# Two transformer layers on one core: jobs of the second layer interleaved into the first

## Chip, core and metric

One Trainium2 chip (trn2), one of its cores. The metric is the device time of one execution in microseconds (us); lower is better. Engines: PE multiplies matrices, DVE and ACT work on vectors, POOL is a slower vector engine, SP only issues DMAs.

## The reference

Four batches x of 256 tokens by 256 channels pass through two layers. LN has no weights; S = 256, D = 256.

```python
# layer 0: 32 query heads on 8 kv heads, head size 8
x = LN(x + softmax(q k^T / sqrt(8)) v Wo)            # q = x Wq, k = x Wk, v = x Wv
x = LN(x + (silu(x G * gs) * (x U * us)) Dn * ds)    # G, U: 256x768, Dn: 768x256, rounded to float8
# layer 1: 16 query heads on 8 kv heads, head size 16, weights transposed
x = LN(x + softmax(q k^T / 4) v wo^T)
g = lut[gate_idx]; u = lut[up_idx]; d = lut[down_idx]    # 688x256, 688x256, 256x688, lut of 16 floats
x = LN(x + (silu(x g^T) * (x u^T)) d^T)
```

## The kernel before

**Jobs.** A job is one batch through one layer: jobs 0 to 3 are layer 0, jobs 4 to 7 layer 1, and job j takes batch j % 4 (`layer`, L53). Job 4 + b needs the output of job b. X (the four batches in fp32) stays on the chip.

**Written orders.** `ORDER` (L68 to L195) holds for PE, ACT, DVE, POOL and SP a list of steps, written out word by word. Each engine runs its list strictly in this order, and steps of different engines are tied by semaphores. A step is `kind.job.part`, and on PE `@n` names one of the three FB banks of PSUM that the step fills. So what an engine does next is fixed; a step whose inputs are late holds up all behind it on its engine.

**The steps of a job, with the lines.**
- `q`, `kv` (PE L948, L966, L971): projections of XT, x transposed, in two buffers; `ldxt` on SP loads them for layer 0, `tr.j.1` (PE L1089, ACT L659) makes them for layer 1 from the finished X. ACT, DVE and POOL split q and k into three bf16 parts (`q`, `qmid`, `kv`, `kmid`), and SP stacks the parts along the partitions (`qstack.j.0` to `.2`, L468, six DMAs; `kstack`, L475, six): QS and KS have NST = 3 buffers, so the stack of job j waits for the scores of job j - 3.
- `max` (PE L992 into MM, DVE L813): the row maxima of the scores, 16 steps a job in layer 0 and 8 in layer 1. There is one MM: the matmuls of a step wait for the reduction of the last. `mt.j.0/1` (DVE L824, L826; PE L1001; ACT L649; SP L511) turns the maxima into two more rows of the stack, for half of the scores each.
- `score` (PE L1024 into SC, ACT L691 exp into PB): 16 or 8 steps, one SC, so the matmuls of one wait for the exp of the last. In layer 0, a step is two matmuls of 512 columns, of two kv groups whose keys lie in partitions 0 to 63 and 64 to 127. PB holds 6 units of exps.
- `pv` (PE L1041 in layer 0, L1050 in layer 1): four strips of 32 rows. Part 0 of a region waits for all the exps of the region (in layer 0 four scores). `stage` (ACT L709), `turn` (PE L1063, DVE L839, L840), `back` (PE L1071, ACT L699): division by the sums, and back.
- `wo` (PE L1080; DVE L851, then the norm's statistics, L772 and L777; POOL L570 to L574 normalizes X). `tr.j.0` (PE L1089, ACT L656, DVE L883) makes XH and XL, the high and low part of the transposed x.
- `gu.j.i.w` (PE L1108): chunk i of six of gate (w = 0) or up (w = 1). Layer 0 has four matmuls in such a step, layer 1 six, since its weights too have a high and a low part. The chunk then goes through ACT (tanh, L682), DVE (L874, L877, into HF, two buffers), ACT (HH, L667) and POOL (HL = HF - HH, `hsplit`, L581).
- `down.j.i` (PE L1119): four matmuls in layer 0, six in layer 1. Its norm is that of `wo`; in layer 0, DVE first multiplies by DS in two instructions (L861).
- `out.j` (SP L527).

**Weights of layer 0's FFN** are rounded through float8 in 12 blocks (`ldq8`, `q8`, `q8w`) into W0. **Weights of layer 1's FFN** are decoded in ten blocks of 432 columns: `ldix` (SP), `lutix` and `lutbits` (ACT, DVE), `lut1` (POOL L599), `lut2` to `lut4` (DVE L919) pick the value by the index bits in LV; `lutlow` copies the high part to W1 (ACT L741), subtracts (POOL L588) and writes the low part to dw in DRAM (SP L523). When all ten are there, `reload` (ACT L742 to L746) fetches dw over W0, once layer 0's FFNs are done: it waits for `down_ready` = 4. The first gu of layer 1 waits for it (`low_in`).

**The places in the orders** that the prediction speaks of. In PE's list before, job 3's FFN stands around max.5.5 and max.5.6, and job 4's begins after max.7.0. In SP's list before: `... qstack.3.2 qstack.3.1 qstack.3.0 mt.1.0 ...` and `... kstack.7.1 lutlow.9 kstack.7.2 mt.6.0 ...`. In ACT's list: `... mt.6.0 reload stage.5.1 score.6.0 ...`.

Of the kernel before, what the change touches and what calls it, by code (L numbers as in the profile page):

```python
# [1175 lines left out]
```

## Time and profile before

| | us |
|---|---|
| median of 3 runs | 384.27 (382.66 to 386.99) |
| the profiled execution | 384.53 |
| its span, first to last instruction | 382.6 |
| PE busy (x instructions) | 309.3 (x2464) |
| DVE busy | 288.5 (x510) |
| ACT busy | 217.0 (x391) |
| POOL busy | 160.9 (x245) |

The granted clock of PE was 0.915 of its full speed over the span; in the slices it is 5 to 9 tenths in the first 155 us and 9 or more behind. Matmuls are pipelined and the records of neighbours overlap, so PE's busy time is more than what its instructions take. A record of a matmul in fp32 comes twice (two passes), of one in fp32r or bf16 once. Times in the rows are us from the start of the span.

### The profile page before, as it was taken

The numbers are of one execution on the slowest core, as the hardware profiler recorded it, in microseconds if no ns is written. First come the engines' busy times: TensorE is split into PE (matmuls) and PEld (weight loads), VectorE is DVE, ScalarE is ACT, GpSimd is POOL, SyncE is SP. The second block draws the span as 40 slices with busy tenths as digits, with TensorE's granted clock in tenths as the row PEclk, the third lists the DMA queues.
The fourth block names the chain that finished last, engine by engine and source line by source line (L and its number), as shares of the span: only waits on it lengthen the run. The fifth ranks groups of instructions, "written<-read, shape, count | busy, mean of one in ns | idle before, by whom it ended". The sixth has DMA issues, their size and how long they took to land.

```text
span 382.6 us, 7048 instructions
## 1 busy us (share of the span) xinstructions
PE 309.3 (81%) x2464; PEld 197.7 (52%) x2464; DVE 288.5 (75%) x510; ACT 217.0 (57%) x391; POOL 160.9 (42%) x245
## 2 busy tenths in 40 slices
...
GB/s 204 291 180 127 148 95 41 40 10 133 14 57 2 11 39 2 69 17 90 2 3 95 55 27 2 78 72 3 10 140 232 3 3 0 3 30 0 29 29 27
DMA packets 23491, 23.06 MB, mean 60 GB/s; under 512 B 3348, under 2 KB 23316, under 8 KB 23328
## 3 DMA queue, kind: packets, MB, share of 16 engines
...
## 4 chain that ended last, share of the span: by engine, by line
PE 39%; DVE 14%; ACT 12%; SPq 12%; issue 10%; POOL 8%; DMA 4%; DVEq 0%; POOLq 0%; ACTq 0%
PE FB L1108 12%; PE FB L1119 7%; PE SC L1024 5%; ACT PB L691 5%; DVE MX L813 5%; SPq L475 4%; SPq L468 4%; PE MM L992 4%; PE FB L1080 3%; PE PV L1041 2%; DVE LV L919 2%; POOL LV L599 2%; POOL X L574 2%; DMA QS<-MP 2%; DVE HF L877 2%
## 5 line engine op out<-in xcount | busy, mean ns | idle before, releaser
L813 DVE TENSOR_REDUCE MX<-MM 128x4 f32<-128x1024 f32 x96 | 117.0, 1219 | 27.9 <-PE MM L992 21.8
L691 ACT ACTIVATE PB<-SC 128x1024 f32<-128x1024 f32 x96 | 98.0, 1021 | 43.9 <-PE SC L1024 40.4
L992 PE MATMUL MM<-KS,QS 62*128 62x256 bf16 (+1 forms) x384 | 48.9, 302 | 26.6 <-DVE MX L813 26.1
L581 POOL TENSOR_TENSOR HL<-HF,HH 128x256 fp32r<-128x256 f32 (+1 forms) x48 | 35.6, 745 | 64.7 <-ACT HH L667 64.4
L599 POOL TENSOR_SCALAR LV<-LB,LD,LT 128x432 f32<-128x432 f32 x80 | 56.2, 717 | 12.8 <-ACT LB L736 12.7
L1024 PE MATMUL SC<-QS,KS 64*128 64x512 bf16 (+1 forms) x192 | 47.6, 418 | 17.3 <-ACT PB L691 11.0
L1108 PE MATMUL FB<-XH,W 128*128 128x256 f32 x288 | 54.8, 299 | 0.2
L992 PEld LDWEIGHTS MM<-KS,QS 62*128 62x128 bf16 (+1 forms) x384 | 20.0, 99 | 55.0 <-DVE MX L813 43.0
L1108 PEld LDWEIGHTS FB<-XH,W 128*128 128x128 f32 x288 | 41.6, 190 | 6.8 <-issue 3.4
L1041 PE MATMUL PV<-PB,VP 128*32 128x256 f32 x512 | 42.3, 433 | 1.9 <-ACT PB L691 1.9
L919 DVE COPY_PREDICATED LV<-LB,LV 128x432 f32<-128x432 uint8 x70 | 42.2, 663 | 2.1 <-POOL LV L599 1.2
L1108 PE MATMUL FB<-XL,W 128*128 128x256 f32 x192 | 38.7, 283 | 0.0
L1024 PEld LDWEIGHTS SC<-QS,KS 64*128 64x128 bf16 (+1 forms) x192 | 10.6, 96 | 43.0 <-ACT PB L691 24.2
L874 DVE SCALAR_TENSOR_TENSOR AA<-TH,FB 128x256 f32<-128x256 f32 (+1 forms) x48 | 19.9, 415 | 15.3 <-ACT TH L682 11.3
L1119 PE MATMUL FB<-W,HH 128*128 128x256 f32 (+1 forms) x144 | 30.2, 307 | 0.4 <-POOL HL L581 0.4
L1108 PEld LDWEIGHTS FB<-XL,W 128*128 128x128 f32 x192 | 29.8, 191 | 0.1
L667 ACT ACTIVATE HH<-HF 128x256 fp32r<-128x256 f32 (+1 forms) x48 | 19.6, 413 | 14.7 <-DVEq L879 12.1
L588 POOL TENSOR_TENSOR LO<-LV,W 128x432 f32<-128x432 f32 x10 | 11.5, 1146 | 38.3 <-ACT W L741 38.3
L1119 PEld LDWEIGHTS FB<-W,HH 128*128 128x128 f32 (+1 forms) x144 | 21.8, 193 | 6.7 <-issue 2.6
L948 PE MATMUL FB<-XT,WQ 128*128 128x256 f32 x64 | 19.3, 448 | 4.1 <-issue 4.1
L574 POOL TENSOR_SCALAR X<-X,NM,RSTD 128x256 f32<-128x256 f32 x32 | 21.2, 670 | 1.7
L1041 PEld LDWEIGHTS PV<-PB,VP 128*32 128x32 f32 x512 | 12.9, 116 | 16.7 <-issue 11.2
...
## 6 DMA issues: line engine op xcount, KB each, us to landing
QS<-QP SPq DMA_DIRECT2D x48, 128.0 KB, 2.4
IX<-in_idx SPq DMA_DIRECT2D x10, 216.0 KB, 3.2
dw<-LO SPq DMA_DIRECT2D x10, 216.0 KB, 1.9
W<-dw ACTq DMA_DIRECT2D x1, 2160.0 KB, 8.8
...
```

Of the source, the lines that this page charges most:

```text
L574: ins = pool.tensor_scalar(X[:, j % B, t, :], X[:, j % B, t, :], NM[:, n % 2, t:t + 1], RSTD[:, n % 2, t:t + 1], ALU.add, ALU.mult)
L581: pool.tensor_tensor(HL[0:r, i, :], HF[0:r, c % 2, :], HH[0:r, i, :].bitcast(F32), ALU.subtract).then_inc(h_parts, 1)
L599: ins = pool.tensor_scalar(LV[:, i, :], LB0[:, :], LD[:, i:i + 1], LT[:, 2 * i:2 * i + 1], ALU.mult, ALU.add)
L691: act.activation(PB[:, unit % PB_UNITS:unit % PB_UNITS + 2, kt, :, :], SC[:, :, :].rearrange("p (f e) s -> p f e s", f=2), ACT.Exp, scale= ...
L813: dve.tensor_reduce(mx, MM[:, :, :].rearrange("p (f i) s -> p f i s", f=2), axis=AX.X, op=ALU.max).then_inc(max_red, 1)
L874: link(dve.scalar_tensor_tensor(out=AA[0:r, :], in0=TH[0:r, (6 * j + i) % 2, :], scalar=1.0, in1=bank[0:r, 0:S], op0=ALU.add, op1=ALU.mult))
L919: ins = dve.copy_predicated(LV[:, i, :], LB[:, k, :], LV[:, i + gap, :])
L992: ins = pe.matmul(MM[:, 2 * f + i, :], QS[lo:lo + r, j % NST, qs + h, qt * P:(qt + 1) * P], keys(j)[lo:lo + r, j % NST, ks, :], start=True ...
L1024: ins = pe.matmul(SC[:, 2 * f:2 * f + 2, :], keys(j)[lo:lo + r, j % NST, ks, kt * P:(kt + 1) * P], QS[lo:lo + r, j % NST, qs + h:qs + h + ...
L1041: ins = pe.matmul(PV[32 * c:32 * c + 32, r % 2, :], VP0[:, j % NST, kt, 4 * (r // 2) + c, w:w + 32], PB[:, (first + c) % PB_UNITS, kt, e, ...
L1108: ins = pe.matmul(bank[:, w * S:(w + 1) * S], ffn_up(l, w, t, i)[part], xs[:, t, :], start=k == 0, stop=k == len(products) - 1)
L1119: ins = pe.matmul(bank[:, t * D:(t + 1) * D], hs[0:rows(l, i), i, t * P:(t + 1) * P], ffn_down(l, i)[part], start=i + k + t == 0, stop=(i, ...
```

## The change

1. Jobs run in the order of `SEQ`: batches 0, 1, 2 of layer 0, batch 0 of layer 1, batch 3 of layer 0, batches 1, 2, 3 of layer 1. So job 3 is now layer 1's batch 0 (it needs job 0), job 4 is layer 0's batch 3, and jobs 5, 6, 7 need jobs 1, 2, 4. All orders are rewritten for it.
2. XT has three buffers.
3. dw is fetched into a tile of its own, W1L, which lies over LV and IX, the scratch of the decoding; `reload` no longer waits for `down_ready`. Q8A and Q8B lie in AA.
4. A score step of layer 0 takes one query head of each of four kv groups: four matmuls of 256 columns. PB holds three quads, and `pv` waits for the exps of its own quad; part order in layer 0 is (quad, kt) instead of (kt, half).

```diff
-PB_UNITS = 6
+PB_QUADS = 3
+SEQ = ((0, 0), (0, 1), (0, 2), (1, 0), (0, 3), (1, 1), (1, 2), (1, 3))
+NXT = 3
 def layer(j):
-    return j // B
+    return SEQ[j][0]
+def batch(j):
+    return SEQ[j][1]
+def earlier(j):
+    return SEQ.index((0, batch(j)))
...
     "PE": (
...
+        "pv.4.3.1 mt.5.0@2 q.6.0@0 score.4.15 q.6.1 back.4.0@2 max.5.5 pv.4.3.2 pv.4.3.3 max.5.6 wo.4.0@1 score.5.0 "
+        "turn.4.1@2 max.5.7 score.5.1 pv.5.0.0 back.4.1@0 score.5.2 pv.5.0.1 mt.5.1@2 wo.4.1 score.5.3 gu.3.0.0@0 "
+        "gu.3.0.1 gu.3.1.0@2 gu.3.1.1 gu.3.2.0@1 gu.3.2.1 gu.3.3.0@0 gu.3.3.1 gu.3.4.0@2 gu.3.4.1 gu.3.5.0@1 gu.3.5.1 "
+        "tr.4.0@0 max.6.0 down.3.0@2 down.3.1 down.3.2 gu.4.0.0@1 gu.4.0.1 down.3.3 down.3.4 max.6.1 score.5.4 "
+        "down.3.5 gu.4.1.0@0 gu.4.1.1 gu.4.2.0@1 gu.4.2.1 gu.4.3.0@2 gu.4.3.1 max.6.2 score.5.5 pv.5.1.0 down.4.0@0 "
+        "gu.4.4.0@1 gu.4.4.1 down.4.1 max.6.3 down.4.2 gu.4.5.0@2 gu.4.5.1 score.5.6 down.4.3 pv.5.1.1 down.4.4 "
+        "score.5.7 max.6.4 turn.5.0@1 down.4.5 pv.5.2.0 pv.5.2.1 pv.5.3.0 pv.5.3.1 max.6.5 mt.6.0@2 back.5.0@0 "
+        "turn.5.1@1 wo.5.0@2 tr.4.1@0 back.5.1@1 max.6.6 score.6.0 q.7.0@0 q.7.1 kv.7.0@1 kv.7.1 max.6.7 score.6.1 "
+        "pv.6.0.0 wo.5.1 score.6.2 mt.6.1@0 pv.6.0.1 score.6.3 pv.6.1.0 pv.6.1.1 max.7.0 tr.5.0@1 score.6.4 "
...
     "ACT": (
...
+        "score.4.14 lutlow.9 mt.5.0 score.4.15 q.6 back.4.0 reload qmid.6 stage.4.1 score.5.0 score.5.1 back.4.1 "
...
     "DVE": (
...
+        "tr.3.0 max.5.3 kv.6 mt.5.0 lut4.9 max.5.4 turn.4.0 max.5.5 q.6 max.5.6 turn.4.1 max.5.7 mt.5.1 wo.4 gu.3.0 "
+        "gu.3.1 gu.3.2 gu.3.3 gu.3.4 gu.3.5 tr.4.0 max.6.0 gu.4.0 max.6.1 down.3 gu.4.1 gu.4.2 max.6.2 gu.4.3 gu.4.4 "
+        "max.6.3 gu.4.5 mt.6.0 max.6.4 down.4 turn.5.0 max.6.5 turn.5.1 max.6.6 q.7 max.6.7 kv.7 mt.6.1 wo.5 max.7.0 "
...
     "SP": (
+        "load.0 ldq8.0 ldq8.1 ldxt.1 load.1 ldix.0 ldxt.2 ldix.1 load.2 ldix.2 qstack.0.0 ldq8.2 ones kstack.0.0 "
+        "qstack.0.1 kstack.0.1 qstack.0.2 kstack.0.2 ldq8.3 ldxt.4 ldix.3 ldq8.4 qstack.1.0 kstack.1.0 kstack.1.1 "
...
+        "mt.1.0 lutlow.3 ldix.7 mt.1.1 lutlow.4 ldix.8 mt.2.0 kstack.3.0 qstack.3.0 qstack.3.1 qstack.3.2 kstack.3.1 "
...
+        "mt.4.1 kstack.6.0 kstack.6.1 kstack.6.2 mt.5.0 lutlow.9 qstack.6.0 qstack.6.1 qstack.6.2 mt.5.1 out.3 mt.6.0 "
+        "qstack.7.0 qstack.7.1 kstack.7.0 qstack.7.2 kstack.7.1 kstack.7.2 mt.6.1 mt.7.0 mt.7.1 out.5 out.6 out.7 "
...
-        XT = sb("XT", [P, 2, DT, S])
-        PB = sb("PB", [P, PB_UNITS, 2, 2, S])
+        XT = sb("XT", [P, NXT, DT, S])
+        PB = sb("PB", [P, PB_QUADS, 2, 4, S])
...
+        spare = ExitStack()
+        LV = spare.enter_context(nc.sbuf_tensor("LV", [P, 8, LUT_W], F32))
+        IX = spare.enter_context(nc.sbuf_tensor("IX", [P, 2, LUT_W], I32))
+        spare.close()
+        W1L = sb("W1L", [P, W1_COLS], F32R)
...
+        def place(j, c):
+            return 2 * (c % 2) + c // 2 if layer(j) == 0 else c
...
                 elif kind == "score":
                     _, j, v = step
-                    unit, kt = unit0(j) + 2 * (v // 2), v % 2
-                    if unit >= PB_UNITS:
-                        act.wait_ge(pv_mm, region_of(unit + 1 - PB_UNITS) + 1)
+                    quad, kt = quad0(j) + v // 2, v % 2
+                    if quad >= PB_QUADS:
+                        act.wait_ge(pv_mm, quad - PB_QUADS + 1)
...
                 elif kind == "reload":
                     act.wait_ge(dw_wr, 16 * N_LUT)
-                    act.wait_ge(down_ready, B)
-                    act.dma_start(W0[:, 0:W1_COLS].bitcast(F32), dw).then_inc(low_in, 16)
+                    act.dma_start(W1L[:, :].bitcast(F32), dw).then_inc(low_in, 16)
...
-                    for f in range(2):
-                        if layer(j) == 0:
-                            g, h = 2 * (2 * (u // 4) + u % 2) + f, 2 * (u // 2 % 2)
-                        else:
-                            g, h = 2 * u + f, 0
-                        lo, ks, qs = stacked(j, g)
-                        ins = pe.matmul(SC[:, 2 * f:2 * f + 2, :],
-                                        keys(j)[lo:lo + r, j % NST, ks, kt * P:(kt + 1) * P],
-                                        QS[lo:lo + r, j % NST, qs + h:qs + h + 2, :], start=True, stop=True)
+                    if layer(j) == 0:
+                        for c in range(4):
+                            lo, ks, qs = stacked(j, 4 * (u // 4) + c)
+                            ins = pe.matmul(SC[:, place(j, c), :], keys(j)[lo:lo + r, j % NST, ks, kt * P:(kt + 1) * P],
+                                            QS[lo:lo + r, j % NST, qs + u % 4, :], start=True, stop=True)
...
                 elif kind == "pv":
...
-                    if part == 0:
-                        pe.wait_ge(exp_done, first + per)
...
+                        e, kt = part // 2, part % 2
+                        quad = quad0(j) + 2 * r + e
...
+                        kt, quad = part, quad0(j) + r
+                    pe.wait_ge(exp_done, 2 * quad + kt + 1)
...
+                    if kt == 1:
+                        ins.then_inc(pv_mm, 1)
```

## Rows read from the trace of the kernel before

**Rows 1.** Page, part 1: busy us (share of the span) and instructions of each engine.

```profile
PE 309.3 (81%) x2464; PEld 197.7 (52%) x2464; DVE 288.5 (75%) x510; ACT 217.0 (57%) x391; POOL 160.9 (42%) x245
```

**Rows 2.** Windows; columns: stretch, length, busy us (x instructions), PEclk, DMA, GB/s.

```profile
24.60:258.00 233.40, 184.22 (x1506) 98.23 (x1506) 200.58 (x334) 152.70 (x264) 100.22 (x142) 0.88 0.19 53
258.00:295.10 37.10, 29.74 (x251) 21.00 (x250) 27.71 (x53) 18.09 (x31) 16.07 (x24) 0.95 0.30 99
295.10:314.00 18.90, 18.62 (x157) 13.86 (x156) 14.79 (x25) 9.96 (x18) 5.09 (x9) 1.00 0.01 3
314.00:375.70 61.70, 61.41 (x507) 53.90 (x505) 30.70 (x76) 26.63 (x57) 25.21 (x45) 1.00 0.04 14
```

**Rows 3.** Chain that ended last, from 340 us on: start, us, what.

```profile
340.35 1.43 PE PV L1050 x24
...
362.49 8.72 PE FB L1108 x72
371.21 4.51 PE FB L1119 x36
...
375.74 0.70 DVE X L864
```

**Rows 4.** Timeline of PE, layer 1: start, us, line, op, tiles, count.

```profile
290.51 0.60 PE L992 MATMUL MM<-KS,QS 96*128 96x256 bf16 x4
...
291.38 1.03 PE L1080 MATMUL FB<-WO,ON 128*128 128x256 f32 x4
```

**Rows 5.** Timeline of PE, layer 0.

```profile
187.93 0.39 PE L992 MATMUL MM<-KS,QS 62*128 62x256 bf16 x4
188.16 0.38 PE L1024 MATMUL SC<-QS,KS 64*128 64x512 bf16 x2
188.47 0.44 PE L1071 MATMUL FB<-IDN,NT 128*128 128x128 f32 x2
```

**Rows 6.** Lines of DVE by form: busy us, mean ns, idle before.

```profile
L813 DVE TENSOR_REDUCE MX<-MM 128x4 f32<-128x1024 f32 x96 | 117.0, 1219 | 27.9 <-PE MM L992 21.8 <-DVE HF L877 3.4
...
L874 DVE SCALAR_TENSOR_TENSOR AA<-TH,FB 128x256 f32<-128x256 f32 x44 | 18.3, 415 | 13.0 <-ACT TH L682 8.9 <-POOL HL L581 2.1 <-DVE HF L877 1.6
...
L861 DVE TENSOR_TENSOR FB<-FB,DS 128x256 f32<-128x256 f32 x8 | 3.0, 421 | 0.3 <-PE FB L1119 0.3
```

**Rows 7.** Timeline of SP at the start.

```profile
14.55 1.95 SPq L468 DMA_DIRECT2D QS<-QP  x3
...
23.43 1.51 SPq L481 DMA_DIRECT2D KS<-KS  x2
```

**Rows 8.** Timeline of SP around mt.1.0 and mt.6.0.

```profile
86.26 3.88 SPq L468 DMA_DIRECT2D QS<-QP  x6
...
285.55 0.67 SPq L511 DMA_DIRECT2D QS<-MP  x1
```

**Rows 9.** Timeline of PE: score.1.0 and score.6.0, idle before in brackets.

```profile
92.90 0.61 PE L1024 MATMUL SC<-QS,KS 64*128 64x512 bf16 x2 [0.96 <-DMA QS<-MP]
...
287.56 1.03 PE L1024 MATMUL SC<-QS,KS 98*128 98x512 bf16 x2 [2.90 <-DMA QS<-MP]
```

**Rows 10.** Waits of PE from 64 to 300 us: total, times, longest.

```profile
PE SC L1024 <- ACT PB L691: 9.4, 18, 1.2
```

**Rows 11.** DMA issues: count, KB each, median us to landing.

```profile
QS<-QP SPq DMA_DIRECT2D x48, 128.0 KB, 2.4
...
dw<-LO SPq DMA_DIRECT2D x10, 216.0 KB, 1.9
W<-dw ACTq DMA_DIRECT2D x1, 2160.0 KB, 8.8
```

**Rows 12.** Timeline of ACT: reload and the step behind it.

```profile
286.46 0.34 ACTq L746 DMA_DIRECT2D W<-dw  x1
286.90 0.60 ACT L709 ACTIVATE ST<-PV 128x512 f32<-128x512 f32 x1 [4.86 <-DMA dw<-LO]
```

**Rows 13.** Timeline of DVE in the FFN block of job 3.

```profile
255.44 0.42 DVE L874 SCALAR_TENSOR_TENSOR AA<-TH,FB 128x256 f32<-128x256 f32 x1 [1.28 <-POOL HL L581]
```

More of the change, by code:

```diff
@@ L45, with later, first @@
 W1_COLS = N_LUT * LUT_W
+SEQ = ((0, 0), (0, 1), (0, 2), (1, 0), (0, 3), (1, 1), (1, 2), (1, 3))
+NXT = 3
 def layer(j):
-    return j // B
+    return SEQ[j][0]
[3 more added lines that the diff above has]
+    return SEQ.index((0, batch(j)))
+def later(j):
+    return SEQ.index((1, batch(j)))
+def first(l):
+    return min(j for j in range(JOBS) if layer(j) == l)
 def halves(j):
@@ L277, in two_layer_kernel @@
         RAW = sb("RAW", [P, 2, Q8_W])
-        Q8A = sb("Q8A", [P, Q8_W], FP8)
-        Q8B = sb("Q8B", [P, Q8_W], FP8)
+        Q8A = AA[:, :].bitcast(FP8)[:, 0:Q8_W]
+        Q8B = AA[:, :].bitcast(FP8)[:, Q8_W:2 * Q8_W]
         BIG = sb("BIG", [P, Q8_W], I32)
@@ L312, in two_layer_kernel @@
         dw = nc.dram_tensor("dw", (P, W1_COLS), F32, kind="Internal").ap()
-        ld_xt = [sem(f"ld_xt{i}") for i in range(2)]
+        ld_xt = [sem(f"ld_xt{i}") for i in range(NXT)]
         ld_w0 = sem("ld_w0")
@@ L392, in stack_count, with xt_count, quad0 @@
             return 16 * NPROD * (j // NST + 1)
+        def xt_count(j):
+            return 16 * sum(layer(i) == 0 for i in range(j % NXT, j + 1, NXT))
         def rows_count(n):
             return 16 * sum(halves(i // 2) for i in range(n % 2, n + 1, 2))
-        def region_of(unit):
-            first = unit0(B)
-            return unit // 4 if unit < first else 4 * B + (unit - first) // 2
+        def quad0(j):
+            return unit0(j) // 2
         def ffn_up(l, which, dt, i):
             o = which * DT * (I0, I1)[l] + dt * (I0, I1)[l] + i * P
-            return (W0[:, o:o + P],) if l == 0 else (W1[:, o:o + P], W0[:, o:o + P])
+            return (W0[:, o:o + P],) if l == 0 else (W1[:, o:o + P], W1L[:, o:o + P])
         def ffn_down(l, i):
@@ L621, in _ @@
                     act.wait_ge(kv_ready, j + 1)
-                    if j in (0, B):
-                        act.wait_ge(ones_pool, 1 if j == 0 else 2)
+                    if j == first(l):
+                        act.wait_ge(ones_pool, l + 1)
                     if j >= NST:
-                        act.wait_ge(pv_mm, 4 * (j - NST + 1))
+                        act.wait_ge(pv_mm, quad0(j - NST + 1))
                     for kt in range(2):
@@ L704, in _ @@
                     n = 2 * j + p
-                    act.wait_ge(pv_mm, 2 * (n + 1))
+                    act.wait_ge(pv_mm, quad0(j) + UNITS[layer(j)] // 4 * (p + 1))
                     if n >= 2:
@@ L937, in _ @@
                     _, j, m = step
-                    l, b = layer(j), j % 2
+                    l, b = layer(j), j % NXT
                     if m == 1:
@@ L1010, in _ @@
                         pe.wait_ge(m_rows[m % 2], rows_count(m))
-                    if v == 0 and j == B:
+                    if v == 0 and j == first(1):
                         pe.wait_ge(ones_in, 16 * 2)
```

92 lines of the change are left out of this document (44 added, 48 removed), and 211 rows, old and new, of the table ORDER.

## The prediction

> **What bounds the kernel now.** I read the page's totals, then a windows view cut at four max steps, then the tail's chain, the timelines around what moves, and the waits. By the page no engine is full: PE 81% of the span, DVE 75% [rows 1]. That is an average over two regimes. To see them I cut where PE starts max.0.0 (24.6 us), max.5.7 (258.0), max.7.0 (295.1) and max.7.7 (314.0) [rows 2]. A, 24.6 to 258.0: DVE busy 200.6 of 233.4 us, PE 184.2. B, to 295.1: DVE 27.7 of 37.1, PE 29.7. C, to 314.0: PE 18.6 of 18.9. D, to 375.7: PE 61.4 of 61.7, DVE half idle. So DVE and the exchange between engines bound A, and PE alone bounds D. A gain lies in PE work that leaves D and finds cover under DVE work. By the written order D holds 38 gu and 24 down steps of layer 1, six matmuls each.
>
> **Prices.** Matmuls overlap, so busy time is no price; I take distances between starts where nothing is waited for. Layer 1: gu 8.72 us for 72 matmuls, 12 steps, = 0.73; down 4.51 for 6 = 0.75; pv 1.43 for 3 = 0.48 [rows 3]; a max and a score step together 0.87 (290.51 to 291.38) [rows 4]. Layer 0: max 0.23, score 0.31 [rows 5]; gu and down, of four matmuls, two thirds of layer 1's. DVE: max 1.22, of which 0.08 lies over its neighbour; an FFN chunk 0.42 and as much again [rows 6]; a norm 1.7 (375.74 to some 377.4 [rows 3]), in layer 0 two multiplies by DS of 0.42 more. PE's small steps are taken in the same way. With these I add up both written orders between the four landmarks, in us of PE work and of DVE work:
> A: before 136 and 193.5, after 132 and 191.6.
> B: before 25.4 and 22.1, after 44.2 and 30.8.
> C: before 16.9 and 13.9, after 15.3 and 11.9.
> D: before 57.7 of PE, after 44.5.
> The totals are the same. The change takes 13 us of PE work out of D (10 gu, 6 down, one each of pv, score, tr, turn) and puts 19 into B, where all of job 3's FFN (12 gu, 6 down of layer 1) and of job 4's (as many of layer 0) now stand.
>
> **A, -5.8.** (1) Order: 191.6 for 193.5 of DVE work at A's own rate, 233.4/193.5 = 1.21: -2.3. (2) Start: SP now issues ldq8.2 and the two `ones` loads between qstack.0.0 and kstack.0.0. Job 0's stack keeps SP busy from 14.55 to 22.3, and max.0.0 starts 2.3 us behind; the `ones` alone take 1.51 [rows 7]. X, 1 MB, also goes out ahead of IX, on whose conversion SP waits. I take +2.5, ends 0 and +5. (3) mt.1.0 stood on SP behind six qstack.3 issues, 86.26 to 90.14 [rows 8], and score.1.0 waited for it until 92.90 [rows 9]; now job 3's stack comes later. PE's own idle was 0.96, the delay 3.88: -2, ends 0 and -3.9. (4) pv now asks for one quad's exps, not for a region's four scores, and an exp's buffer is free after one pv_mm of its own quad. From 64 to 300 us PE waited 9.4 us for exps ahead of scores [rows 10]. Ends 0 and -9.4; -4, nearer none, since a score still waits for the one SC. (5) Layer 0's score step is now four matmuls of 256 columns over two row groups, not two of 512. Its like is layer 0's max, 0.23 from start to start against 0.31 [rows 5]: 0, ends -5 (64 x 0.08) and, if the row groups ran one after the other at twice 0.23, +10 of PE time, most of it under DVE. (6) The third XT buffer, Q8A and Q8B in AA and W1L in LV and IX add no instruction and, with the orders as written, no wait of their own (AA's first gu comes long after q8.11, and reload waits for dw anyway): 0.
>
> **B, +17.4.** PE's 44.2 exceed DVE's 30.8: the stretch turns from DVE-bound to PE-bound. At D's rate, 61.7/57.7, put at 1.06: 46.9. Two stalls on top.
> First, `reload`. From lut4.9 on: ACT's copy 0.6, POOL 1.15, SP 0.6 to 1.3, landing in dw 1.9, then 2160 KB in 8.8 [rows 11]: 13.4 us. PE's list from there to gu.3.0.0 holds 7.4 us of work, four scores with their exps in series among it, some 10.5 in all: a stall of 2.5, ends 0 and 6. Queued behind gu.3.0.0 are max.6.0 and all of PE, and DVE waits for both. Today PE doesn't wait for these weights, though ACT stood 4.86 us for dw [rows 12]. The wait for down_ready goes, as W1L is not W0; only so can reload come ahead of job 3's FFN.
> Second, job 7's chain, which now hangs on job 4. From down.4.5: DVE's norm 2.6, POOL's 2.4, then tr.4.1, with turn.5.0 (and so back.5.0) behind that norm; PE has 3.9 us of steps ahead of tr.4.1, so 2 with the hand-overs. Then q.7 to max.7.0: twelve stack issues at 0.65 (six in 3.88 [rows 8]) from q_hi on, which is 2.4 us in, and 2.4 of landing [rows 11]: 12.6. PE's q and kv, and three scores with their exps, fill some 9.5: 3.1. Together 5.1, ends 2 and 8. Behind max.7.0 stand tr.5.0 and gu.5, so all of PE waits here too.
> B after: 46.9+2.5+5.1 = 54.5, against 37.1. The 2.90 us ahead of score.6.0, for mt.6.0 behind kstack.7 on SP [rows 8, 9], are in the 37.1 only: mt.6.0 now precedes qstack.7.0.
>
> The new reload runs on ACT's queue while SP sends six qstack.6 loads of 128 KB; beside today's there are none. If they share the engines' time, reload lands later by what the stacks move: 768 KB at 2160/8.8 = 245 KB/us, 3.1 us [rows 11]. That is the third rival. The Trainium skill ("DMA: Bandwidth & Descriptors", Queues, rings and completion order) says that each DMA engine goes round its queues packet by packet, which would make it so; no stretch of this trace shows it for the reload.
>
> **C, -1.8; D, -12.8.** C: 15.3 at today's 18.9/16.9 = 17.1. D: 44.5 at 1.065 = 47.4, and 1.5 for tr.6.0, over whose norm (DVE 1.7, POOL 2.4, hand-overs) only 3.9 us of PE steps lie: 48.9 against 61.7. The chain through mt.7.1, four scores, pv, turn, wo, tr and gu.7 needs some 37, so it is no bound. Behind the last matmul nothing changes: 6.9 us to the end of the span.
>
> **The sum.** -5.8+17.4-1.8-12.8 = -3.0. The profiled execution took 384.53 (its span 382.6 and 1.9 around it); the median of the runs is 384.27. So 381.5 for such an execution and 381.2 for the median, -0.8%. Under 1%, 3.8 us, is about what a measurement of this kernel can't tell from no change.
>
> **Rivals.**
> First, the moved work hides. PE is idle for 49 us of A, DVE for 9 of B [rows 2]. If B's FFN steps fill waits rather than add to them, B grows by 10, not 17.4: 373.8; at the most all of D's 12.8 is gained, 371.5. For it: D runs gap-free with the same steps. Against: the twelve gu steps of job 3 stand in one block with no max between, so DVE starves. The Trainium skill ("Perfetto Trace Analysis", Identifying the Most-Contended Engine) says that interleaving regimes with different busiest engines may help; it doesn't say by which of the two prices.
> Second, slower: in B the hand-over of FFN chunks sets the pace, not PE. A chunk goes PE, ACT, DVE (0.42 twice), ACT, POOL, over three banks and two HF buffers, with maxes of 1.22 between on DVE; layer 0's costs PE only 0.96. It decides from a rate of 1.13 in B on (3.0/44.2 above 1.06), where the gain is gone. Today's B ran at 37.1/25.4 = 1.46, stalls and all; midway, at 1.25, it costs 8.4: 389.6. For it: DVE waited 1.28 us for POOL's HL in the like block at 255 [rows 13]. Against: D has the same hand-over and runs at 1.07.
> Third, reload lands 3.1 us later: 384.3, no change.
> Fourth, the change doesn't do what it says, in that the scores' row groups lose their overlap: +10 of PE time, a fifth of which A lets through: 383.2.
>
> **Chances.** Forecast 0.42, first rival 0.26, second 0.18, third 0.09, fourth 0.05. The forecast's own range is 377 to 386; as it lies near the 1% bound (380.4), 0.17 of it is faster, 0.23 same, 0.02 slower. First: 0.24 faster, 0.02 same. Second: 0.14 slower (over 388.1), 0.04 same. Third and fourth: 0.01 faster, 0.11 same, 0.02 slower. Faster 0.42, same 0.40, slower 0.18. The range goes from the first rival's full hiding, 371, to just past the second, 391.
>
> **What would show it.** Right: the last max starts at 323 to 328 (today 314) and PE is solid for 48 to 50 us behind it; gu.3.0.0 waits 1 to 4 us for reload; max.7.0 waits 2 to 4 for stack 7; score.1.0 no longer waits for rows; layer 0's score steps stand 0.23 to 0.31 apart. Wrong: A is shorter by over 10 us; or B takes under 47 us (the work hid) or over 58 (the hand-over or reload decides). DVE's idle time ahead of max.6.x and its releaser tell which.

## The result, and the profile after

| | before | after |
|---|---|---|
| median of the runs, us | 384.17 (4 runs) | 397.65 (396.14 to 399.94, 4 runs) |
| ratio, 95% interval | 1 | 1.034 (1.029 to 1.039) |
| the profiled execution, us | 384.53 | 397.33, span 395.5 |

The change made the kernel 3.4% slower; the forecast was 381.2 in a range of 371 to 391. The time is outside the range and on the other side of 1.

The page of after, part 1 (compare [rows 1]), and part 2's row of the granted clock in 40 slices of 9.9 us:

```profile
PE 313.6 (79%) x2592; PEld 199.1 (50%) x2592; DVE 285.0 (72%) x510; ACT 217.1 (55%) x391; POOL 161.5 (41%) x245
...
PEclk9966558798699989999999999996999989999998
```

The totals hardly moved: DVE has 3.5 us less, PE 4.3 more, the span is 12.9 longer. So the time is in waits and in where they lie. The clock row has two dips behind 155 us, in slices 28 and 33, which [rows 2] don't have to that depth (0.95 and 1.00).

The windows of after, cut where PE starts the same four steps as in [rows 2] (max.0.0, max.5.7, max.7.0, max.7.7):

```profile
28.20:261.60 233.40, 182.83 (x1615) 95.08 (x1616) 201.09 (x336) 147.51 (x255) 106.04 (x147) 0.89 0.19 53
261.60:320.60 59.00, 50.70 (x396) 39.39 (x394) 33.23 (x70) 28.05 (x53) 19.48 (x35) 0.94 0.22 68
320.60:339.60 19.00, 18.24 (x140) 13.89 (x140) 12.77 (x20) 8.84 (x15) 1.46 (x2) 0.92 0.01 2
339.60:388.60 49.00, 48.10 (x394) 40.82 (x392) 23.67 (x60) 21.30 (x46) 20.25 (x36) 1.00 0.04 13
```

Against the stretches of before:

| | before | after | moved by | forecast |
|---|---|---|---|---|
| up to max.0.0 | 24.6 | 28.2 | +3.6 | +2.5, told in A |
| A | 233.4 | 233.4 | 0 | -8.3 (-5.8 with the start) |
| B | 37.1 | 59.0 | +21.9 | +17.4 |
| C | 18.9 | 19.0 | +0.1 | -1.8 |
| D | 61.7 | 49.0 | -12.7 | -12.8 |
| sum | | | +12.9 | -3.0 |

The sum misses by 15.9: 9.4 of it ahead of the end of A, 4.5 in B, 1.9 in C, 0.1 in D. The first cut of before was taken a little early: its PE starts max.5.7 at 258.38, not at 258.0. So 0.4 us of A stand in B in the column of before, and by the exact cut A lost 0.4 and B gained 22.3; the tables and sums below keep 258.0.

**Where B's time went.** The timeline of PE in after, at the first gu of layer 1 (columns as in [rows 4], the idle time before in brackets):

```profile
270.51 0.77 PE L1139 MATMUL FB<-XH,W 128*128 128x256 f32 x2 [3.59 <-DMA W1L<-dw]
271.08 0.63 PE L1139 MATMUL FB<-XH,W1L 128*128 128x256 f32 x2
271.51 0.63 PE L1139 MATMUL FB<-XL,W 128*128 128x256 f32 x2
...
275.35 0.63 PE L1139 MATMUL FB<-XL,W 128*128 128x256 f32 x2
275.77 0.50 PE L1139 MATMUL FB<-XH,W 128*128 128x256 f32 x2
276.11 0.40 PE L1139 MATMUL FB<-XH,W1L 128*128 128x256 f32 x2
276.35 0.40 PE L1139 MATMUL FB<-XL,W 128*128 128x256 f32 x2
```

Read the distances between starts. Behind a wait of 3.59 us for the reload, a pair of matmuls takes 0.43 us; from 276.11 on it takes 0.235. The first twelve pairs (270.51 to 275.77, 5.26 us) thus cost 12 x (0.43 - 0.235) = 2.3 us more than the same work behind them. Windows of these 5.26 us and of as many behind them say why (PEclk is the third column from the end):

```profile
270.51:275.77 5.26, 5.26 (x24) 5.26 (x25) 0.85 (x2) 0.38 (x1) 0.31 (x1) 0.50 0.02 6
276.10:281.30 5.20, 5.20 (x47) 5.20 (x46) 3.08 (x8) 2.68 (x8) 2.45 (x4) 1.00 0.00 0
```

The granted clock is 0.50, the lower of PE's two levels (1.2 of 2.4 GHz), and then 1.00. It fell during PE's wait of 3.59 us, over which it is 0.81 on average. The wait costs 5.9, not 3.6.

The kernel before has the same thing, at its wait of 2.90 us ahead of score.6.0. The prediction's rows show it: two matmuls of 512 columns of that step take 1.03 us [rows 9], while four of 256 columns at the end of the slow stretch take 0.60 [rows 4]. The window of the 3 us from score.6.0 on:

```profile
287.50:290.50 3.00, 2.94 (x12) 2.43 (x13) 0.56 (x2) 1.30 (x3) 0.00 (x0) 0.50 0.89 317
```

The reload itself, and the queue beside it (DMA issues, as in [rows 11]; then SP's timeline and ACT's issue):

```profile
W1L<-dw ACTq DMA_DIRECT2D x1, 2160.0 KB, 10.9
```

```profile
258.03 5.01 SPq L502 DMA_DIRECT2D QS<-QP  x6
...
259.45 0.34 ACTq L782 DMA_DIRECT2D W1L<-dw  x1
```

It landed in 10.9 us where 8.8 was seen in [rows 11], and the six qstack issues beside it took 5.01 where six took 3.88 [rows 8]. That W1L is another tile than W0 isn't the reason: in the run code_only below, the same transfer into W1L has no stack loads beside it and lands in 9.0 (in one profiled execution, of 389.31 us).

PE and DVE at the second place, max.7.0, the first step of job 7:

```profile
316.12 0.61 PE L1063 MATMUL SC<-QS,KS 98*128 98x512 bf16 x2 [0.54 <-ACT PB L729]
...
317.90 0.64 PE L1083 MATMUL PV<-PB,VP 128*32 128x256 f32 x8 [0.60 <-ACT PB L729]
320.62 1.01 PE L1028 MATMUL MM<-KS,QS 96*128 96x256 bf16 x4 [2.09 <-issue]
321.43 1.06 PE L1120 MATMUL FB<-IDN,X 128*128 128x128 f32 x4
322.28 1.06 PE L1063 MATMUL SC<-QS,KS 98*128 98x512 bf16 x2
```

And DVE's own timeline at that place:

```profile
321.74 1.23 DVE L849 TENSOR_REDUCE MX<-MM 128x4 f32<-128x1024 f32 x1 [5.43 <-PE MM L1028]
```

PE waits 0.54 + 0.60 + 2.09 us around job 7's stack, and again the steps behind it are slow: 1.01 and 1.06 us where 0.60 stands in [rows 4]. "issue" names no releaser. SP's last three stack loads of job 7 were issued from 317.29 to 319.13, and such loads take some 2 us to land, so the stack is most likely what came last. DVE idles 5.43 us for it.

**Where A's time did not go.** Waits of PE in after, 64 to 300 us, as in [rows 10]. The scores of layer 0 and of layer 1 now have a line each, which before was one:

```profile
PE SC L1058 <- ACT PB L729: 9.5, 13, 1.8
PE SC L1063 <- ACT PB L729: 0.6, 3, 0.2
```

10.1 us, against 9.4 before: the finer release of the exps, put at -4, bought nothing.

DVE is busy for 201.1 us of A; before, 200.6 [rows 2], although the prediction counted 1.9 us less work. That is a matter of the cut. PE and DVE don't reach a step together: before, PE started max.5.7 at 258.38 and DVE reduced it only at 262.22, behind gu.3.4, gu.3.5, lutbits.9 and turn.4.0 (3.33 us busy from 258.0 to 262.22). In after, PE starts it at 261.59 and DVE reduces it at 262.75, with only turn.4.1 between. Cut at DVE's own max.0.0 and max.5.7, before and after:

```profile
25.00:262.22 237.22, 188.07 (x1548) 101.36 (x1548) 203.91 (x343) 153.98 (x267) 102.19 (x145) 0.88 0.18 52
29.18:262.75 233.57, 183.18 (x1616) 95.34 (x1616) 201.27 (x338) 147.25 (x251) 106.18 (x147) 0.90 0.19 54
```

DVE did lose 2.6 us of work and comes through its part 3.6 us faster, but PE gets none of it: between PE's own two starts A is as long as before.

At score.1.0, whose wait for rows (0.96 us [rows 9]) is gone, PE now waits one step earlier and longer, for DVE's reduction of max.1.9, ahead of which DVE's list has mt.1.0 and wo.0:

```profile
96.41 0.61 PE L1028 MATMUL MM<-KS,QS 62*128 62x256 bf16 x4 [2.42 <-DVE MX L849]
97.15 0.61 PE L1058 MATMUL SC<-QS,KS 64*128 64x256 bf16 x4
```

PE starts score.1.0 27.4 us behind max.1.0 (69.75); before, it was 27.2 (92.90 behind 65.73).

### The profile page after: what moved, and what is told of

Its sections match the earlier page's. It is cut to its first block, busy times and chain, and to the rows that moved or that the text cites. A ratio compares the mean times of both kernels' runs of the same rounds, so it can differ in the third digit from the quotient of the medians.

```text
span 395.5 us, 7309 instructions
## 1 busy us (share of the span) xinstructions
PE 313.6 (79%) x2592; PEld 199.1 (50%) x2592; DVE 285.0 (72%) x510; ACT 217.1 (55%) x391; POOL 161.5 (41%) x245
## 4 chain that ended last, share of the span: by engine, by line
PE 38%; DVE 17%; issue 11%; ACT 9%; SPq 8%; POOL 8%; DMA 8%; DVEq 0%; POOLq 0%; ACTq 0%
PE FB L1139 12%; PE FB L1150 6%; DVE MX L849 5%; ACT PB L729 4%; PE MM L1028 3%; SPq L509 3%; DMA W1L<-dw 3%; POOL X L608 3%; PE SC L1058 3%; PE PV L1083 3%; PE FB L1111 2%; DVE HF L913 2%; POOL LV L633 2%; DMA IX<-in_idx 2%; DVE LV L955 2%
## 5 line engine op out<-in xcount | busy, mean ns | idle before, releaser
L1083 PE MATMUL PV<-PB,VP 128*32 128x256 f32 x768 | 62.3, 405 | 2.6 <-ACT PB L729 2.3
L1139 PE MATMUL FB<-XH,W 128*128 128x256 f32 x192 | 44.0, 312 | 4.1 <-DMA W1L<-dw 3.6
L955 DVE COPY_PREDICATED LV<-LB,LV 128x432 f32<-128x432 uint8 x70 | 43.2, 678 | 0.2
L1139 PEld LDWEIGHTS FB<-XH,W 128*128 128x128 f32 x192 | 31.3, 199 | 12.2 <-issue 7.5
L1058 PE MATMUL SC<-QS,KS 64*128 64x256 bf16 x256 | 27.0, 292 | 12.4 <-ACT PB L729 10.7
L1139 PEld LDWEIGHTS FB<-XL,W 128*128 128x128 f32 x192 | 30.9, 198 | 0.0
L1083 PEld LDWEIGHTS PV<-PB,VP 128*32 128x32 f32 x768 | 16.5, 110 | 25.1 <-issue 16.6
L1058 PEld LDWEIGHTS SC<-QS,KS 64*128 64x128 bf16 x256 | 8.3, 96 | 30.5 <-ACT PB L729 22.7
L720 ACT ACTIVATE TH<-FB 128x256 f32<-128x256 f32 (+1 forms) x24 | 9.2, 382 | 26.3 <-PE FB L1139 26.2
L1150 PE MATMUL FB<-W,HH 128*128 128x256 f32 (+1 forms) x96 | 21.6, 307 | 1.1 <-DVEq L916 1.0
L984 PE MATMUL FB<-XT,WQ 128*128 128x256 f32 x64 | 20.3, 466 | 0.5 <-DVE QR L826 0.5
## 6 DMA issues: line engine op xcount, KB each, us to landing
W1L<-dw ACTq DMA_DIRECT2D x1, 2160.0 KB, 10.9
```

Source lines behind the costliest of these rows:

```text
L955: ins = dve.copy_predicated(LV[:, i, :], LB[:, k, :], LV[:, i + gap, :])
L984: ins = pe.matmul(bank[:, m * S:(m + 1) * S], WQ[l][:, t, m:D:2], XT[:, b, t, :], start=t == 0, stop=t == DT - 1)
L1058: ins = pe.matmul(SC[:, place(j, c), :], keys(j)[lo:lo + r, j % NST, ks, kt * P:(kt + 1) * P], QS[lo:lo + r, j % NST, qs + u % 4, :], star ...
L1083: ins = pe.matmul(PV[32 * c:32 * c + 32, r % 2, :], v, PB[:, quad % PB_QUADS, kt, place(j, c), :], start=part == 0, stop=part == (3, 1)[la ...
L1139: ins = pe.matmul(bank[:, w * S:(w + 1) * S], ffn_up(l, w, t, i)[part], xs[:, t, :], start=k == 0, stop=k == len(products) - 1)
L1150: ins = pe.matmul(bank[:, t * D:(t + 1) * D], hs[0:rows(l, i), i, t * P:(t + 1) * P], ffn_down(l, i)[part], start=i + k + t == 0, stop=(i, ...
```

## The experiments

All ratios are to runs of the kernel before on the same chip in the same rounds.

**The new code under the old orders (code_only).** `SEQ` is the natural order and all lists are those of before, while quads, buffers and W1L are the change's.

```diff
-SEQ = ((0, 0), (0, 1), (0, 2), (1, 0), (0, 3), (1, 1), (1, 2), (1, 3))
+SEQ = ((0, 0), (0, 1), (0, 2), (0, 3), (1, 0), (1, 1), (1, 2), (1, 3))
 ORDER = {
-    ...
+    the lists of the kernel before
```

> The changed code (score quads, one quad's exps ahead of pv, three XT buffers, W1L over the scratch, reload without down_ready) under the old job order and all five old written orders. Theory 1 (the job order with its written orders is what costs; the code is neutral): 382 to 386 us, A (first max to max.5.7) 231 to 235 us. Theory 2 (the quads cost: four short matmuls a score, more wait handling ahead of pv, and this ate the gain forecast for A): 388 us or more, A at 238 or more.

388.01 us, ratio 1.003 (0.999 to 1.007). The median is outside the 382 to 386 of the first theory and at the bound of the second, but the kernel before ran at 385.43 on this chip, so the ratio decides: by its interval the code costs 0.7% at the most and gains 0.1%, and most of the 3.4% comes from the orders. The -4 for quads goes. The fourth rival, the lost overlap of row groups, was priced at 2 us or 0.5%, which this interval doesn't exclude; the trace of after does. A score step of layer 0 stands 0.32 us ahead of the next step, where 0.31 was seen before [rows 5] and 0.46 would be twice 0.23:

```profile
255.86 0.39 PE L1058 MATMUL SC<-QS,KS 64*128 64x256 bf16 x4
256.18 1.14 PE L984 MATMUL FB<-XT,WQ 128*128 128x256 f32 x4
```

**The reload in two DMAs (split_reload).** The first brings what gate and up read, the second what down reads, which waits for it separately.

```diff
-act.dma_start(W1L[:, :].bitcast(F32), dw).then_inc(low_in, 16)
+cut = 2 * DT * I1 + P
+act.dma_start(W1L[:, 0:cut].bitcast(F32), dw[:, 0:cut]).then_inc(low_in, 16)
+act.dma_start(W1L[:, cut:].bitcast(F32), dw[:, cut:]).then_inc(low_in2, 16)
...
+                    if j == first(1) and i == 0:
+                        pe.wait_ge(low_in2, 16)
```

> The changed kernel, with the reload issued as two DMAs, the gate and up columns first with a semaphore of their own; the down columns are waited for before down.3.0. Theory 1 (the stall ahead of gu.3.0.0 costs twice: 3.6 us of waiting and some 3.3 us because PE's granted clock is at the lower level for the next five gu steps): the load of the first part lands in some 7 us instead of 10.9, gu.3.0.0 starts 3.5 us sooner without a wait, its steps take 0.72 at once, total 391 us. Rival (the FFN block is bound by its hand-overs, the stall is hidden by what comes later, at max.7.0): 396 or more.

393.72 us, ratio 1.022 (1.016 to 1.028), so 1.2% of the 3.4 are gone; the time lies between the theory's 391 and the rival's 396. DMA issues and PE's timeline of this kernel:

```profile
W1L<-dw ACTq DMA_DIRECT2D x1, 1440.0 KB, 6.8
W1L<-dw ACTq DMA_DIRECT2D x1, 720.0 KB, 9.2
```

```profile
267.11 0.59 PE L1142 MATMUL FB<-XH,W 128*128 128x256 f32 x2
267.53 0.40 PE L1142 MATMUL FB<-XH,W1L 128*128 128x256 f32 x2
267.77 0.40 PE L1142 MATMUL FB<-XL,W 128*128 128x256 f32 x2
```

No bracket stands behind the first row: no wait, and no slow pairs. B is 52.4 long, 6.6 less than after's, which is the 5.9 read above and little else. C grew from 19.0 to 20.3 with a granted clock of 0.85, since the wait at max.7.0 is still there; part of the gain was lost to it.

**Filler matmuls in the reload's wait (warm).** The reload stays whole; thirty matmuls into a bank that the first gu then overwrites keep PE busy up to it.

```diff
+                            if j == 3:
+                                for n in range(30):
+                                    pe.matmul(bank[:, 0:S], W1[:, 0:P], XH[:, n % 2, :], start=True, stop=True)
                             pe.wait_ge(low_in, 16)
```

> The changed kernel, with 30 matmuls of 256 columns (some 3.6 us) that write what gu.3.0.0 then overwrites, put between score.5.3 and the wait for reload. The wait stays. Theory 1 (clock): gu.3.0.0 starts at the same time within 0.5 us, its first five steps take 0.72 and not 1.1 to 1.4 each, total 394.5. Rival (those steps are slow because something else holds them, the reload's DMA or the first weights): no step is faster, total 397.5 or more.

396.73 us, ratio 1.029 (1.024 to 1.034); by the median 0.5% below the change, with intervals that overlap, and between the theory's 394.5 and the rival's 397.5. The trace shows the mechanism where the median is weak:

```profile
267.52 3.94 PE L1134 MATMUL FB<-XH,W 128*128 128x256 f32 x30
271.30 0.40 PE L1142 MATMUL FB<-XH,W 128*128 128x256 f32 x2
271.53 0.40 PE L1142 MATMUL FB<-XH,W1L 128*128 128x256 f32 x2
```

The weights came no sooner than in the change (271.3 against 270.5), but the pairs are 0.235 apart from the first on. From the first gu to max.6.0 PE took 8.9 us instead of 11.4. So the two costs are separate: 3.6 for the wait and, by this run, 2.5 for the clock behind it (2.3 by the pairs above).

**SP's start as before (start_order).** IX's loads ahead of load.1, ldq8.2 and the ones behind job 0's stack.

```diff
-load.0 ldq8.0 ldq8.1 ldxt.1 load.1 ldix.0 ldxt.2 ldix.1 load.2 ldix.2 qstack.0.0 ldq8.2 ones kstack.0.0 qstack.0.1 kstack.0.1 ...
+load.0 ldq8.0 ldq8.1 ldxt.1 ldix.0 ldix.1 load.1 ldxt.2 load.2 ldix.2 qstack.0.0 kstack.0.0 kstack.0.1 qstack.0.1 ... ldq8.2 ones
```

> The changed kernel, with SP's list at the start as it was in the kernel before: IX ahead of X, ldq8.2 and ones behind job 0's stack. Theory 1: max.0.0 starts 3 us earlier (25.2 instead of 28.2) and all of it stays, as DVE bounds what follows: 394.5. Rival (the late start is given back in A, since max.5.7 is paced by the decoding): 397 to 398.

398.67 us, ratio 1.035 (1.029 to 1.041): no gain, a miss; the rival was nearer. PE started max.0.0 at 25.3 instead of 28.2, but max.1.0 at 69.8 instead of 69.7. DVE's list has q8.2 ahead of max.0.0, and its load was now late:

```profile
25.35 0.36 DVE L933 TENSOR_SCALAR BIG<-RAW 128x384 int32<-128x384 int32 x1 [8.74 <-DMA RAW<-in_gate]
```

**SP's, DVE's and ACT's start together (start_both).** The same, with q8.2 behind kv.1 in DVE's list and behind q.1 and kv.1 in ACT's.

```diff
-DVE: ... q8.1 q8.2 q.1 max.0.0 kv.1 q8.3 max.0.1 ...
+DVE: ... q8.1 max.0.0 q.1 kv.1 q8.2 max.0.1 lut2.0 q8.3 ...
-ACT: ... lutbits.0 q8.2 q.1 kv.1 q8w.2 ...
+ACT: ... lutbits.0 q.1 kv.1 q8.2 q8w.2 ...
```

> The changed kernel, with job 0's start put back in three lists at once: SP sends IX ahead of X and ldq8.2 and ones behind job 0's stack; DVE takes q8.2 and q8.3 behind max.0.0 and max.0.1 instead of ahead of them; ACT takes q.1 and kv.1 ahead of q8.2. Theory (the written order of job 0 on DVE, where max.0.0 stands behind q8.2, is what lost 4 us at max.1.0 and made the run start_order lose what it gained): max.0.0 at 25.3, max.1.0 at 66.5 to 67.5 instead of 69.7, total 394.5 to 395.5. Rival (job 0 is bound by its DVE work, start or not): max.1.0 at 69 or later, total 397 or more.

401.06 us, ratio 1.038 (1.032 to 1.044): a second miss, and again the rival's side. DVE now waited at max.0.0 itself, for job 0's stack:

```profile
25.75 1.22 DVE L849 TENSOR_REDUCE MX<-MM 128x4 f32<-128x1024 f32 x1 [9.53 <-PE MM L1028]
```

What DVE doesn't do ahead of the stack, it has to do later: max.1.0 started at 70.9, later than in the change itself. The earliest max.0.0 isn't the best start. Why max.4.0 to max.5.0 then took 52.3 us instead of 48.6 I can only say from the clock, 0.86 from 190 to 215 us where the change has 1.00; what lowered it stays open.

**Split reload and fillers ahead of max.7.0 (split_warm7).** Eighteen matmuls into MM behind the last reduction and ahead of the wait for job 7's stack.

```diff
+                    if j == 7 and u == 0:
+                        pe.wait_ge(max_red, unit0(j) + u)
+                        for n in range(18):
+                            pe.matmul(MM[:, 0, :], W1[:, 0:P], XH[:, n % 2, :], start=True, stop=True)
                     if u == 0:
                         pe.wait_ge(q_in[j % NST], stack_count(j))
```

> As split_reload, and 18 matmuls of 256 columns (some 2.1 us) into MM, which max.7.0 then overwrites, ahead of the wait for job 7's stack. Theory (a wait of 2 us there lowers PE's granted clock for the next steps, and C, at 20.3 us for 15.3 of work, pays for it): max.7.0 starts at the same time within 0.5 us, C takes 17.5 to 18.5 us, total 391.5 to 392.5. Rival (C is bound by DVE's reductions and exps, the clock doesn't matter): C stays at 20, total 393.5 or more.

391.69 us, ratio 1.013 (1.007 to 1.019), as the theory said. Windows of B and C:

```profile
264.20:316.70 52.50, 50.04 (x415) 39.30 (x413) 33.23 (x70) 27.61 (x53) 19.44 (x35) 1.00 0.23 74
316.70:334.50 17.80, 17.06 (x143) 12.85 (x142) 12.70 (x20) 8.85 (x15) 1.46 (x2) 1.00 0.01 2
```

The clock is 1.00 throughout, and C is 17.8 instead of 20.3. B and C together are 70.3 us against the change's 78.0 and the 56.0 of before. Job 7's stack is still waited for, now under 2.4 us of fillers; without them the sum would be 67.9, and still 11.9 above before. So without the two stalls B and C still take back nearly all of D's 12.7, and the later start is on top. By the prices, B and C have 17.2 us of PE work more than before; 11.9 of it shows in the time.

**Half of the gu work left out, in A and in B (trim_a, trim_b).** Both on top of the last kernel: in one the gu steps of jobs 0, 1 and 2, all in A, take only the first half of the 256 input channels; in the other those of jobs 3 and 4, all in B.

```diff
+                    full = len(products)
+                    if j in (0, 1, 2):          # the other kernel: (3, 4)
+                        products = [q for q in products if q[2] == 0]
```

> split_warm7 with the gu steps of jobs 0, 1 and 2 (all in stretch A) cut to half of their matmuls: the second half of the 256 input channels is left out, 36 steps x 2 matmuls x 0.12 us = 8.6 us of PE work gone from A. split_warm7 measured 391.7 (1.0134). If PE work in A lies under DVE's (201 busy of 233 us), as the price of nothing for the four us that left A says, A loses under 2 us: 390 to 392. Rival: A is set by the exchange PE-DVE in series, so PE work counts there at half or more: 383 to 387. A lower granted clock because PE does less could also make it slower, up to 393.

> split_warm7 with the gu steps of jobs 3 and 4 (all in stretch B) cut to half in the same way: 12 steps x 3 matmuls (layer 1) and 12 x 2 (layer 0), 60 x 0.12 = 7.2 us of PE work gone from B. If B is PE-bound, it loses nearly all of it: 385 to 386 (1.000 of the kernel before). Rival, the hand-over of FFN chunks or DVE's maxes set B's pace: the time stays within 2 us of split_warm7's 391.7.

In A: 391.93 us, ratio 1.020 (1.014 to 1.026); the median didn't fall, and the profiled A went from 235.7 to 233.2 us for 8.6 us of PE work taken away. PE work in A is nearly free, so the 4 us that the change took out of A could buy little.

In B: 389.76 us, ratio 1.012 (1.007 to 1.017), and the profiled B fell by 1.6, to 50.9: of 7.2 us of PE work, under a quarter came back. My expectation missed. Timeline of PE, DVE and POOL inside job 3's block in that kernel:

```profile
271.51 0.39 PE L1149 MATMUL FB<-XH,W 128*128 128x256 f32 x1 [0.39 <-DVEq L919]
...
272.71 0.39 PE L1149 MATMUL FB<-XH,W 128*128 128x256 f32 x1 [0.22 <-DVEq L919]
...
273.69 0.42 DVE L913 SCALAR_TENSOR_TENSOR AA<-TH,FB 128x256 f32<-128x256 f32 x1 [1.19 <-POOL HL L616]
...
274.79 0.39 PE L1149 MATMUL FB<-XH,W 128*128 128x256 f32 x1 [1.09 <-DVEq L919]
```

From the fourth chunk on PE now waits for DVE's release of the FB bank. Chunks come 1.20 us apart, and once 2.08, when POOL is at the norm of X and HL is late; from the first gu to max.6.0 it took 7.9 us. With all matmuls PE alone needs 1.42 a chunk, 9.1 us up to max.6.0, and it runs that block without a gap. So PE does set the pace of job 3's block, but the hand-over lies right behind it: the second rival's mechanism is there, one step down. In the rest of B the 2.9 us left out of job 4's gu bought 0.4; which step took their place there I haven't followed up. The price of PE work in B holds for work added to it, not for work taken out.

**The kernel before with what it waited for moved away (old_unblocked).** Here I left the change and asked which of its ideas were good alone: mt.1.0 ahead of the qstack.3 issues, mt.6.0 behind kstack.7.0 on SP, the reload split, and behind stage.5.1 and score.6.0 in ACT's list.

```diff
-SP:  ... lutlow.2 qstack.3.2 qstack.3.1 qstack.3.0 mt.1.0 ldix.6 ...
+SP:  ... lutlow.2 mt.1.0 qstack.3.2 qstack.3.1 qstack.3.0 ldix.6 ...
-SP:  ... kstack.7.0 qstack.7.2 kstack.7.1 lutlow.9 kstack.7.2 mt.6.0 mt.6.1 ...
+SP:  ... kstack.7.0 mt.6.0 qstack.7.2 kstack.7.1 lutlow.9 kstack.7.2 mt.6.1 ...
-ACT: ... mt.6.0 reload stage.5.1 score.6.0 back.5.0 ...
+ACT: ... mt.6.0 stage.5.1 score.6.0 reload back.5.0 ...
```

> The kernel before, job order untouched, with the waits that the trace shows taken out by small moves: mt.1.0 ahead of qstack.3 and mt.6.0 behind kstack.7.0 on SP, stage.5.1 and score.6.0 ahead of reload on ACT, reload in two DMAs. Theory (these rows come late and hold all of PE): score.1.0 1.5 to 2 us and score.6.0 2.5 us earlier, total 380 to 382. Rival (a step that comes earlier in A or B only waits longer for DVE later): 383.5 to 385.

381.51 us, ratio 0.987 (0.983 to 0.992): it beats both kernels. Windows of B, C and D:

```profile
257.40:291.40 34.00, 28.12 (x249) 19.56 (x248) 27.35 (x52) 17.88 (x30) 15.79 (x23) 1.00 0.28 88
291.40:311.10 19.70, 18.87 (x158) 13.83 (x157) 14.89 (x26) 9.97 (x18) 5.11 (x9) 1.00 0.09 37
311.10:372.70 61.60, 61.30 (x507) 53.82 (x505) 30.64 (x76) 26.66 (x57) 25.31 (x45) 1.00 0.04 14
```

B is 3.1 us shorter than in [rows 2], 2.7 by the exact cut at 258.38. The waits of PE's scores for rows of maxima, 6.1 us over the span of the kernel before (2.90 of them at score.6.0 [rows 9]), are down to:

```profile
PE SC L1027 <- DMA QS<-MP: 2.0, 3, 0.8
```

The reload is late here too, but costs only this:

```profile
292.48 0.71 PE L1111 MATMUL FB<-XH,W 128*128 128x256 f32 x4 [0.55 <-DMA W<-dw]
```

**Its parts (old_mt1, old_reload).** mt.1.0 alone, and the reload alone (split, and moved in ACT's list):

> The kernel before with one edit, mt.1.0 ahead of the six qstack.3 issues in SP's list (the step that the prediction put at -2, ends 0 and -3.9). Theory: worth the prediction's value, 0.3 to 0.7% faster (383 to 381.5 beside 384.3). Rival: the wait of score.1.0 lies beside DVE work in a stretch that DVE sets, and the time stays within 0.2%.

> The kernel before with the reload in two DMAs and behind stage.5.1 and score.6.0 in ACT's list, mt.1.0 and mt.6.0 left where they are. ACT then doesn't stand 4.86 us for dw ahead of two steps that PE and DVE wait for. Theory: ACT's wait held PE, 2 to 3 us gone: 0.5 to 0.8% faster. Rival: score.6.0 then waits on mt.6.0 (behind kstack.7 on SP, 2.90 us) all the same, and the time stays within 0.3%.

mt.1.0 alone: 382.66 us, ratio 0.991 (0.987 to 0.995). The forecast's -2 for this edit was right in sign and, at 1.9 to 5.0 us by the interval, not too large; the gain is above the 0.3 to 0.7% expected of this run, but the intervals overlap. The reload alone: 384.71, ratio 0.998 (0.994 to 1.002), nothing to be told from none. The rival of that run held: score.6.0 waited all the same for the mt rows, which on SP stand behind kstack.7:

```profile
284.18 1.04 PE L1027 MATMUL SC<-QS,KS 98*128 98x512 bf16 x2 [2.67 <-DMA QS<-MP]
```

The 4.86 us for which ACT stood for dw [rows 12] lay beside that wait of PE, and by the ratio taking them away bought 0.6% at the most. mt.6.0 was not run by itself; that it brings the rest of the 1.3% is the difference of the three runs, not a measurement.

**The change's start put into the kernel before (old_slowstart).**

```diff
-SP: load.2 load.0 ldq8.0 ldq8.1 ldxt.1 ldix.0 ldix.1 load.1 ldix.2 ldxt.2 qstack.0.0 kstack.0.0 ... ldix.3 ldq8.2 ones ldq8.3
+SP: load.0 ldq8.0 ldq8.1 ldxt.1 load.1 ldix.0 ldxt.2 ldix.1 load.2 ldix.2 qstack.0.0 ldq8.2 ones kstack.0.0 ... ldix.3 ldq8.3
```

> The kernel before with only the first lines of SP's list as the change has them: X loaded ahead of IX (load.0 first, load.1 ahead of ldix.0, load.2 late), ldq8.2 and the two ones between qstack.0.0 and kstack.0.0. Theory, the prediction's step (start +2.5): max.0.0 starts 2 to 4 us later than the 24.6 of before, and the whole delay reaches the end: 386.5 to 388, ratio 1.006 to 1.010. Rival, suggested by start_order, where a max.0.0 that was 2.9 us earlier left max.1.0 where it was: stretch A evens it out, max.1.0 stays at 65.7 to 66.3 and the ratio within 0.3% of 1.

387.80 us, ratio 1.003 (0.999 to 1.007): inconclusive for a cost of 0 to 2.6 us. The profiled execution was the longest of the twelve (390.52 us). In its trace max.0.0 started 2.6 us late (27.2), which is the forecast's term, and max.1.0 1.2 late (66.9 for 65.7). So one trace suggests, and the ratio doesn't contradict it, that a late first step isn't passed on in full. In the change it was: +3.6 at max.0.0 and +4.0 at max.1.0 (69.7), +3.3 at max.3.0, +3.2 at max.5.7.

## Why the prediction was wrong

**Right.** The cut into four regimes; D, -12.8 forecast and -12.7 measured, with PE solid in 49.0 us (48 to 50 were named); the direction and the main size of B (most of the added PE work is paid, and PE runs job 3's block without a gap); gu.3.0.0's wait (1 to 4 named, 3.59 read) and max.7.0's (2 to 4 named, 3.2 read with the two gaps ahead of it); mt.1.0's gain as an edit by itself, as its own run shows; score steps without a cost for row groups (0.32). Of the signs of being wrong one came up: B took 59.0 us, over the 58 named.

**A, step (1), the order, -2.3.** The count of 1.9 us less DVE work was sound; DVE's own windows show 2.6. The step that failed was to turn it into time between PE's starts of two max steps: the work that went had stood between PE's max.5.7 and DVE's, outside A as it was timed. Within A DVE is busy 201.1 us against 200.6, and A is 233.4 both times. The PE work that left A was nearly free where it was: half of three jobs' gu could be left out without a shorter median.

**A, step (4), the exps, -4.** I had taken a wait of 9.4 us as something that a finer release could shorten. It measured 10.1 after, and the code under the old orders ran at 1.003. A score waits for its one SC, as the working itself objected; the value should have been the end at 0.

**A, steps (2) and (3).** The start was 3.6 rather than 2.5, within its ends. mt.1.0's gain is real in the old order, and in the change score steps wait 1.1 us for such rows in all, against 6.1 in the kernel before. But A as a whole didn't get shorter by it. At score.1.0 itself the wait for rows only made room for one of 2.42 us for DVE; what took the gain back over the rest of A I haven't isolated. The two trials at the start show that an edit of a few us there is evened out or turned around before max.1.0. So of the 9.4 us missed ahead of B, by the forecast's own terms, 6.3 are steps 1 and 4, 1.1 is the start, and 2 are step 3, the only one whose cause stays open.

**B, the reload term, 2.5.** It measured 5.9 by two parts. The wait was 3.6; the landing was 2.1 later than the 8.8 in the row, next to six stack loads that took 5.01 instead of 3.88 themselves. That is the third rival's mechanism, at two thirds of its 3.1; the shared use of the DMA engines that the Trainium skill states ("DMA: Bandwidth & Descriptors", Queues, rings and completion order) agrees with it. The other 2.3 wasn't in the forecast at all: PE's steps behind the wait ran at the lower clock, as the forecast's own rows showed for score.6.0. The split and the fillers show both parts.

**B, the job 7 term, 5.1.** PE waited 3.2, less than put down, but the same clock cost follows, and falls into C: 19.0 or 20.3 with the wait, 17.8 with fillers. So of C's miss of 1.9, 1.2 is the clock (19.0 against 17.8) and 0.7 the rate.

**B, the rate of 1.06.** 59.0 less 5.9 and 3.2 leaves 49.9 for 44.2 us of priced work, a rate of 1.13; the kernel with fillers, less 2.4 of filler and the two gaps of 0.54 and 0.60, has 49.0, or 1.11. D's rate was too good for a stretch with maxima and exps in it: 3.0 us. The three B terms add to the miss: 3.4 - 1.9 + 3.0 = 4.5.

**The rivals.** Most of the moved work didn't hide (first): 14.3 us more for B and C even when repaired. The second was priced from a rate of 1.13 on, and B's rate was that, but not by its mechanism as far as the traces show: in job 3's FFN block PE had no gap. The hand-over bounds what a lighter PE could get, 1.20 us a chunk. The third was right in part. None ended at 397: the slower side was priced as one mechanism, while the actual loss was a forecast gain in A that wasn't there (9.4), a rate taken from D that B didn't have (3.0), and two stalls that cost about one and a half times their length (3.6 became 5.9; 3.2 became 4.4).
